# Decoder layer with a mixture of experts: dense routed experts replaced by tokens scattered by expert into 15 tiles

## The reference, cut to what matters

```
shared = einsum(silu(x @ sw_gate) * (x @ sw_up), sw_down)                  # sw_gate, sw_up: 256 x 704
probs  = softmax(x @ router_w.T);  top_w, top_i = top_k(probs, 2)          # 8 experts, two per token
combine = sum(one_hot(top_i, 8) * (top_w / sum(top_w))[..., None])
h = silu(einsum('th,ehi->eti', x, w_gate)) * einsum('th,ehi->eti', x, w_up)   # e = 8, i = 176
routed = einsum('eth,te->th', einsum('eti,eih->eth', h, w_down), combine)
out = x + routed + sigmoid(x @ shared_gate_w)[:, None] * shared
```

## Time and profile before

| what | us |
|---|---|
| median of 3 runs | 638.91 |
| the three runs | 642.28, 638.73, 638.91 |
| span of the profiled execution | 636.7 |
| the profiled execution's own time, taken as the median | 638.9, 2.2 of it around the span |
| group 0's mixer, with no FFN beside it | 0 to 131 |
| mixers of groups 1, 2 and 3, each with an FFN beside it | 131 to 279, 279 to 426, 426 to 572 (ends rounded) |
| tail: the rest of the FFN of group 3 | 572 to 636.7 |

### The profile page before, as it was taken

One profiled execution on the slowest core, in us unless ns is written; L12 is line 12 of the kernel. 1 busy time (PEld: TensorE's weight loads), 2 busy tenths in 40 slices (PEclk: granted clock), 3 DMA queues, 4 the chain that ended last, 5 costly groups with the idle time before them and its releaser, 6 DMA issues.

```text
span 636.7 us, 15520 instructions
## 1 busy us (share of the span) xinstructions
PE 599.7 (94%) x6307; PEld 483.6 (76%) x6307; DVE 409.6 (64%) x841; ACT 278.9 (44%) x637; POOL 342.8 (54%) x462
## 2 busy tenths in 40 slices
PE   7987967979999999999999999999999999999997
PEld 6544545636988889755888889864898888899997
DVE  5997897778744755869644755869762655752221
ACT  4867224232335556342435555251435555343332
POOL 7684145247446667614456666615364666519766
PEclk9999999979999999999999999999999999999999
DMA  8931000020121121011021111002011112014320
GB/s 189 343 104 35 1 1 4 0 68 6 39 67 39 43 60 43 14 34 51 30 80 36 39 52 49 23 17 69 18 51 34 39 44 60 29 38 123 97 55 16
DMA packets 41824, 34.08 MB, mean 54 GB/s; under 512 B 9901, under 2 KB 41206, under 8 KB 41754
## 3 DMA queue, kind: packets, MB, share of 16 engines
q1 hardware_dynamic: 39850, 31.27, 18.2%
q10 hardware_dynamic: 1904, 1.84, 0.9%
HBM read 30.92 MB, written 2.17 MB: 52 GB/s over the span
## 4 chain that ended last, share of the span: by engine, by line
PE 37%; DVE 25%; POOL 13%; issue 9%; ACT 9%; SPq 1%; DMA 1%; POOLq 0%; ACTq 0%; DVEq 0%
DVE A L1574 7%; DVE nm L1652 5%; PE bank L1040 5%; POOL hb L625 3%; PE bank L1237 3%; POOL A L714 3%; PE bank L1044 3%; PE bank L1045 3%; PE bank L1046 3%; PE bank L1084 3%; POOL hT L614 2%; PE bank L1164 2%; POOL hT_last L723 2%; PE bank L1086 2%; PE bank L1085 2%
## 5 line engine op out<-in xcount | busy, mean ns | idle before, releaser
L614 POOL TENSOR_TENSOR hT<-hb,hT 128x256 fp32r<-128x256 f32 (+1 forms) x102 | 78.0, 765 | 72.0 <-ACT hT L789 72.0
L625 POOL TENSOR_TENSOR hb<-hb,cwb 128x256 f32<-128x256 f32 (+1 forms) x102 | 77.0, 755 | 68.6 <-DVE hb L1549 68.5
L1549 DVE TENSOR_TENSOR hb<-hb,bank 128x256 f32<-128x256 f32 (+1 forms) x102 | 42.7, 418 | 101.6 <-ACT hb L799 101.6
L789 ACT ACTIVATE hT<-hb 128x256 fp32r<-128x256 f32 (+1 forms) x102 | 42.4, 416 | 126.0 <-POOL hb L625 125.8
L1044 PE MATMUL bank<-xTf,wGh 128*128 128x256 f32 x272 | 82.9, 305 | 0.0
L1574 DVE TENSOR_TENSOR A<-bank,decay 128x512 f32<-128x512 f32 x128 | 77.4, 682 | 6.0 <-PE bank L1153 5.9
L1045 PE MATMUL bank<-xTf,wGh 128*128 128x256 f32 x272 | 76.7, 282 | 0.0
L1046 PE MATMUL bank<-xTf,wGl 128*128 128x256 f32 x272 | 76.5, 281 | 0.0
L1045 PE MATMUL bank<-xTf,wUh 128*128 128x256 f32 x256 | 72.2, 282 | 0.0
L1046 PE MATMUL bank<-xTf,wUl 128*128 128x256 f32 x256 | 72.1, 282 | 0.0
L1044 PE MATMUL bank<-xTf,wUh 128*128 128x256 f32 x256 | 72.1, 282 | 0.0
(11 more groups left out here) (230 smaller groups left out, 1418.3 us busy)
## 6 DMA issues: line engine op xcount, KB each, us to landing
cwb<-cw_rows SPq DMA_DIRECT2D x54, 128.0 KB, 2.9
A<-cw_rows SPq DMA_DIRECT2D x18, 128.0 KB, 4.0
A<-in_x SPq DMA_DIRECT2D x4, 512.0 KB, 4.3
res<-in_x SPq DMA_DIRECT2D x4, 512.0 KB, 4.8
out_x<-res SPq DMA_DIRECT2D x8, 256.0 KB, 2.4
rawG<-in_L_ffn_w_gate SPq DMA_DIRECT2D x2, 704.0 KB, 6.6
rawU<-in_L_ffn_w_up SPq DMA_DIRECT2D x2, 704.0 KB, 6.6
cwb<-cw_rows SPq DMA_DIRECT2D x12, 112.0 KB, 2.6
```

Of the source, the lines that this page charges most:

```text
L614: pool.tensor_tensor(hT[hr, c % 2, 1, :], hb[hr, c % 2, :], hT[hr, c % 2, 0, :].bitcast(F32), ALU.subtract).then_inc(h_lo, 1)
L625: pool.tensor_tensor(hb[hr, c % 2, :], hb[hr, c % 2, :], cwb[hr, c % CWS, :], ALU.mult).then_inc(h_scaled, 1)
L789: act.activation(hT[hidden(n), c % 2, 0, :], hb[hidden(n), c % 2, :], ACT.Copy).then_inc(h_hi, 1)
L1549: tt(h, h, up_part(PS[5 + c % 2], n), ALU.mult).then_inc(gu_used, 1)
```

## The change

The routed experts are no longer computed for all tokens. A group's 512 tokens have 1024 choices of an expert; each choice gets a row in a table `xs_rows` in device memory (HBM) of RT = 15 tiles of 128 rows, ordered by expert, each expert's share rounded up to whole tiles (15 tiles hold any outcome of the routing). For that, PE counts each token's rank within its expert (`rank_tokens`, 8 small matmuls), DVE turns ranks and counts into row numbers `pos` and a table `tab` of each tile's expert (`place_tokens`, nine small operations after the second scores step), and POOL scatters the normed tokens by 8 indirect DMAs (`scatter`, two behind each of the receptances 4 to 7). PE loads the 15 experts into registers once a group (`load_experts`), and addresses the expert's weights by them.

A routed tile goes: SP loads 128 rows (`load_tile`), PE turns them (2 transposes, L1257), ACT makes the high (L922), DVE the low part (L1790); PE makes gate and up at once with the tokens as the stationary operand (6 matmuls of 352 columns, L1270 to L1272); ACT silu (L928), DVE product (L1811, L1812); PE turns the product (L1286, L1287), ACT makes the high (L934), DVE the low part (L1796); PE multiplies by the down weights (5 matmuls of 256 columns, L1298 to L1302); ACT takes the result out (L941), SP stores it to `ys_rows`. At the end POOL gathers each token's two rows by 8 indirect DMAs (`gather`), and DVE adds them with their weights (`routed_out`, 8 operations). The POOL multiplication by routing weights and the DMAs of `cw_rows` go.

The shared expert stays as before, in 12 items. A group now has 27 items and 30 ticks: shared items at ticks 0 to 5 and 22 to 27, tiles at ticks 7 to 21, which is `n4` to `x3a`. `COUNT` puts one tick instead of two at `x{b}a`. Within the mixers the down product of a tile follows one tick behind its gate and up (`down_lag` 1, shared items still 2), in the tail two. Other moves: the receptance buffer `rbd` lies in the memory of `hT`, the context in that of `hb`, POOL makes seven more constants at the start, and a DMA fills `xs_rows` with zeros once. Line numbers from L1100 on in the quoted pieces are those of the changed kernel.

```diff
-    FN = 2 * FB
-    TICKS = FN + 2
+    SFB = -(-SI // P)
+    FN = 2 * SFB
+    RT = 2 * GT // P + E - 1
+    NI = FN + RT
+    TICKS = NI + 3
...
-        COUNT = dict(n0=1, n1=2, n2=2, n3=2, n4=1, n5=1, y0=2, r0=2, r1=1, r2=1, r3=1)
...
+        COUNT = dict(n0=1, n1=2, n2=2, n3=2, n4=1, n5=1, y0=2, r0=1, r1=1, r2=1)
...
-            for p, k in (("a", 2), ("b", 1), ("c", 2)):
+            for p, k in (("a", 1), ("b", 1), ("c", 2)):
...
+            def load_tile(f, r):
+                if r >= 2:
+                    sp.wait_ge(xt_turned, f * RT + r - 1)
+                sp.dma_start(ring[:, r % 2, :], xsD[r * P:(r + 1) * P, :]).then_inc(xs_in[r % 2], 16)
...
+            def scatter(f, q):
+                k, b = q // GB, q % GB
+                if q == 0:
+                    pool.wait_ge(slots_ready, f + 1)
+                    if f == 0:
+                        pool.wait_ge(zero_out, 16)
+                    else:
+                        pool.wait_ge(xs_in[0], 16 * loads_before(f, 0))
+                        pool.wait_ge(xs_in[1], 16 * loads_before(f, 1))
+                pool.indirect_dma_start(out=xsD, out_offset=bass.IndirectOffsetOnAxis(ap=pos[:, k, b:b + 1], axis=0),
+                                        in_=tok2[:, b, :], in_offset=None).then_inc(scattered, 16)
...
+                if n >= TICKS - 4:
+                    gather(f, 2 * (n - TICKS + 4))
+                    gather(f, 2 * (n - TICKS + 4) + 1)
...
+                    if g and u >= 4:
+                        scatter(g - 1, 2 * (u - 4))
+                        scatter(g - 1, 2 * (u - 4) + 1)
...
+            def ffn_tick(f, n, exp_next=False):
+                if high_late(f, n):
+                    high_part(f, shared_at(f, n - 1))
+                if tile_at(f, n) is not None:
+                    tile_high(f, tile_at(f, n))
+                if down_lag(f) == 1 and routed_at(f, n, 1) is not None:
+                    hidden_high(f, routed_at(f, n, 1))
+                if routed_at(f, n) is not None:
+                    silu_routed(f, routed_at(f, n))
+                elif shared_at(f, n) is not None:
+                    silu_shared(f, shared_at(f, n))
+                if exp_next:
+                    act.activation(spare, mhalf[:, 0:1], ACT.Exp).then_inc(exp_table, 1)
+                if down_lag(f) == 2 and routed_at(f, n, 1) is not None:
+                    hidden_high(f, routed_at(f, n, 1))
+                if routed_at(f, n, down_lag(f)) is not None:
+                    take_out(f, routed_at(f, n, down_lag(f)))
...
+            def gate_up_routed(f, r, e):
+                c, t = f * NI + routed_item(f, r), slice((r % 2) * P, (r % 2 + 1) * P)
+                pe.wait_ge(gu_used, c - 1)
+                if f + 1 < NG and r >= 2:
+                    pe.wait_ge(y_out, f * RT + r - 1)
+                pe.wait_ge(xt_hi, f * RT + r + 1)
+                pe.wait_ge(xt_lo, f * RT + r + 1)
+                o = PS[5 + c % 2][:, 0:2 * I].rearrange("p (w n) -> p w n", w=2)
+                for k in range(KC):
+                    ws = bass.ds(e * I, I)
+                    mm(o, xTf[:, 0, k, t], wH[:, :, k, ws], start=k == 0, stop=False, skip_group_check=True)
+                    mm(o, xTf[:, 1, k, t], wH[:, :, k, ws], start=False, stop=False, skip_group_check=True)
+                    last = mm(o, xTf[:, 0, k, t], wL[:, :, k, ws], start=False, stop=k == 1, skip_group_check=True)
+                last.then_inc(gu_ready, 1)
...
+            def down_routed(f, r, e):
+                c = f * NI + routed_item(f, r)
+                if f == 0 and r == 0:
+                    pe.wait_ge(f_hi, SPLITS)
+                    pe.wait_ge(f_lo[1], len(FW) + len(DOWN_PIECES))
+                pe.wait_ge(r_lo, f * RT + r + 1)
+                if r and f + 1 == NG:
+                    pe.wait_ge(y_out, f * RT + r)
+                h2, o = hT[:, c % 2], PS[y_bank(f, r)][:, 0:C]
+                mm(o, h2[:, 0, 0:P], wDf[:, bass.ds(e * C + DH * C, C)], start=True, stop=False, skip_group_check=True)
+                mm(o, h2[:, 1, 0:P], wDf[:, bass.ds(e * C + DH * C, C)], start=False, stop=False, skip_group_check=True)
+                mm(o, h2[:, 0, 0:P], wDf[:, bass.ds(e * C + DL * C, C)], start=False, stop=False, skip_group_check=True)
+                mm(o, h2[0:I2, 0, P:2 * P], wDf[0:I2, bass.ds(e * C + DM * C, C)], start=False, stop=False, skip_group_check=True)
+                mm(o, h2[0:I1, 1, P:2 * P], wDf[0:I1, bass.ds(e * C + DM * C, C)], start=False, stop=True,
+                   skip_group_check=True).then_inc(down_done, 1)
...
             def ffn_tick(f, n):
+                if n == R0[f] - 1:
+                    load_experts(f)
+                if tile_at(f, n) is not None:
+                    turn_tile(f, n)
+                if down_lag(f) == 1 and routed_at(f, n, 1) is not None:
+                    turn_hidden(f, routed_at(f, n, 1))
+                r = routed_at(f, n)
+                if r is not None:
+                    gate_up_routed(f, r, expert_of[f][r])
+                elif shared_at(f, n) is not None:
+                    gate_up(f, shared_at(f, n))
+                if down_lag(f) == 2 and routed_at(f, n, 1) is not None:
+                    turn_hidden(f, routed_at(f, n, 1))
+                r = routed_at(f, n, down_lag(f))
+                if r is not None:
+                    down_routed(f, r, expert_of[f][r])
+                if n >= 2 and shared_at(f, n - 2) is not None:
+                    down(f, shared_at(f, n - 2))
...
+            def tile_low(f, r):
+                dve.wait_ge(xt_hi, f * RT + r + 1)
+                t = slice((r % 2) * P, (r % 2 + 1) * P)
+                tt(xTf[:, 1, :, t], PS[xt_bank(f, r)][:, 0:KC * P].rearrange("p (k t) -> p k t", k=KC), xTf[:, 0, :, t].bitcast(F32),
+                   ALU.subtract).then_inc(xt_lo, 1)
+
+            def hidden_low(f, r):
+                c = f * NI + routed_item(f, r)
+                dve.wait_ge(h_hi, c + 1)
+                tt(hT[:, c % 2, 1, :], PS[ht_bank(f, r)][:, 0:2 * P], hT[:, c % 2, 0, :].bitcast(F32), ALU.subtract).then_inc(r_lo, 1)
...
+                if n == SFB + 1:
+                    shared_out(f, 0)
+                if tile_at(f, n) is not None:
+                    tile_low(f, tile_at(f, n))
+                if down_lag(f) == 1 and routed_at(f, n, 1) is not None:
+                    hidden_low(f, routed_at(f, n, 1))
+                r = routed_at(f, n)
+                if r is not None:
+                    c = f * NI + routed_item(f, r)
                     dve.wait_ge(silu_done, c + 1)
-                    h = hb[hidden(n), c % 2, :]
-                    tt(h, h, up_part(PS[5 + c % 2], n), ALU.mult).then_inc(gu_used, 1)
+                    h, up = hb[:, c % 2, :], PS[5 + c % 2][:, I:2 * I]
+                    both = h[:, P:P + I2].rearrange("p (w n) -> p w n", w=2)[:, ::-1, :]
+                    tt(h[:, 0:P], h[:, 0:P], up[:, 0:P], ALU.mult)
+                    tt(both, h[:, P:I].unsqueeze(1).to_broadcast([P, 2, I1]), up[:, P:I].unsqueeze(1).to_broadcast([P, 2, I1]),
+                       ALU.mult).then_inc(gu_used, 1)
...
+                    if g and u == 1:
+                        place_tokens(g - 1)
...
+                if g:
+                    routed_out(g - 1, 0)
+                    routed_out(g - 1, 1)
...
-            for n in range(4, AHEAD):
-                gate_up(NG - 1, n)
-            for n in range(FN):
-                if n + AHEAD < FN:
-                    gate_up(NG - 1, n + AHEAD)
-                down(NG - 1, n)
+            for n in range(TICKS):
+                ffn_tick(NG - 1, n)
...
+            place_tokens(NG - 1)
+            for n in range(TICKS):
+                ffn_tick(NG - 1, n)
+            routed_out(NG - 1, 0)
+            routed_out(NG - 1, 1)
```

667 lines of the change are left out of this document (406 added, 261 removed).

## The result

The changed kernel takes 757.25 us in the median of 4 runs (751.06 to 760.04), the kernel before 640.6 (638.73 to 643.61): ratio 1.180, 95% interval 1.173 to 1.187. Forecast were 713, slower.

The account below looks back on a forecast made before the run. PE's matmuls were taken as the bound before the change. Base 636.7 + 58.5 (three middle groups) + 2.0 (start) + 14 (tail) = 711.2 span, plus 2.2 to the median: 713 us; 8-in-10 range 645 to 785.

Parts of the forecast that it names:

- about 19 us a batch, limited by the way through the four engines: X phase: each batch grows from 16.1 to about 19 us, with PE waiting on work passing through the other engines.
- another 1.0: X batch, after the first tick behind the keys: PE's next turning waits 1.0 us for DVE's product.
- the clock: X phase: PE's waits lower its clock, a batch goes to about 26 us; 797, or 755 if half do; chance 0.13.
- 2.08: PE's price in us for one routed tile: six 352-column matmuls, five of 256 columns and four transposes.
- The 1.0 taken: N phase: PE's loading of 15 registers once a group costs 1.0 us, within bounds of 0 and 2.9.
- the 1.2 taken: Scores: one scatter holds POOL 1.2 us, within bounds of 0.39 and 2.9, costing +0.6 for the phase.
- rival 4: A scatter or gather holds POOL the whole 2.9 us, in scores and tail: 780; chance 0.08.
- +2.0: Start: seven more constants on POOL ahead of the decay's cut, 0.29 each, lengthen the start by 2.0 us.
- six shared items to 580: Tail: PE works through six shared items until 580 us while the eight scatters run, also to 580.
- Scores, n and r phase: Additions per middle group: scores +2.0 for placing and +0.6 for scatters, n phase +2.0, r phase +3.9.
- the right sign: X batches of 17 to 21 us, PE idle about 5 us in each; tail's first tile about 21 us after routing starts.
- the wrong signs: X batches under 15 us, PE over 90% busy or clock 0.50 through the x phase, or receptances waiting for POOL's scatters.

Follow-up runs that it names:

- the first experiment: Changed kernel with the hidden tile's turning and high and low parts in each x batch's first tick issued ahead of the previous batch's attention: 729.1 us.
- the fixed experts: Changed kernel with tile r always taking expert r modulo 8, without register loads and address instructions: 749.0 us.
- the full rows: Changed kernel with a tile's last two down matmuls on all 128 rows, not 96 and 48, using the first part's weights: 736.9 us.

## Why the prediction was right, and where its sizes were off

**The direction and the mechanism.** The step "about 19 us a batch, limited by the way through the four engines" came out as 20.6, with its two waits at the named instructions, 2.19 and 1.75 against 2.5 and 1.9; the third, "another 1.0", was 0.3. The three middle groups gave +84 against +58.5. The x batches carry the larger share of this difference: 21.0 against 15.9 before, each on the mean of nine, 5.0 more where the forecast had 2.9 (19 against 16.1), which in these nine makes 19 of the 26 us. With the waits filled and the clock at 1.00 a batch took 19.3. That this is so near 19 is partly luck: four tiles cost 1.1 more than was taken, and the three waits 1.2 less.

**The clock.** It was made a rival, "the clock", that was to bring 7 us per batch; the sum had nothing for it in the x phase. It lies between: in group 2's batches the waits of 2.2 were followed by 0.50, but for some 3 us only, and filling the waits gave 1.7 per batch. The argument by length of wait (1.8 left it at 1.00, 2.5 might not) did not hold up: in the first experiment waits of 1.74 were followed by 0.50 in six of nine batches.

**The price of a tile.** The term "2.08" is 2.35 in the tail, without waits; the fixed experts show that registers have no part in it, the full rows that the change of rows does: it costs 0.35, and the rest of a tile came out 0.08 cheaper than forecast. 0.27 for 60 tiles is 16 us of PE's time. With it the gain of PE is 46.6 - 35.3 = 11.3 per group and not 15.4.

**Registers.** The 1.0 taken is not seen on PE. By the Trainium skill ("Runtime: NRT & Kernel Launch", section "Instruction fetch mechanics") a register takes about 200 ns to load, which gives an estimate of 3.0 us a group for 15; this trace does not show it: the turning behind the load starts 0.12 after the matmul ahead of it. Leaving the loads out brought 8 us in all, which no row assigns to them.

**Scatters.** A scatter holds POOL 0.98 and 0.30 until the next, 1.28 against the 1.2 taken. PE waited for a receptance only once, 1.2 us, so rival 4, POOL's queue, didn't come.

**Start.** "+2.0" was 9.8. Up to the last of group 0's maxima it was 3.8 (97.2 before, 101.1 now), where the sum had 2.0 for the constants. Of the other 6.0, DVE's norm beside POOL's splits and receptances takes 4.7: the step left out that the receptances, free of their old buffer, no longer wait.

**Tail.** 18.6 against 14. The step "six shared items to 580" beside the scatters failed: their low parts wait on POOL behind all eight, 7.6 us of PE, and moving them gave 8 back. The first tile came 25.4 us after the routing's first step, where 21 was the sign.

**Scores, n and r phase** were forecast at 8.5 together. The way from the routing to the first maxima grew by 5.5 to 9.3 and that from the last maxima to the routing by 4.4 to 6.1, the latter with most of the last batch in it. Between the first score product (L1395) and the query projection (L1500) lie 9.2, 6.2 and 4.0 of it, where scores and n phase had 4.6. PE's wait ahead of the scores was 3.44 against 3.7, but not where the forecast had it: the rank matmuls (L1341) did not wait in groups 1 and 2; the projection ahead of them (L1187) waits for DVE's addition of the values (L1730), which stands behind the additions of the gathered rows and the routing:

```profile
317.43 3.68 PE L1187 MATMUL bank<-A,wA 128*128 128x512 f32 x4 [3.44 <-DVE A L1730]
```

Moving half of that addition shortened the wait and left the median as it was. The rest was not taken apart by a run of its own, and its causes stay open.

**Sums.** Some sums of the forecast are slightly off, with no weight in the result: three batches of 19 and one of 17 make 74 and not 75.5, 648 is 11.3 over 636.7 and not 11.5, and with batches of 13.8 the sum would give 651 and not 653.

**The signs.** Three of the nine batches are over the 21 of the right sign, PE is idle 4.1 in a batch and not 5, and none of the wrong signs came: PE is busy 80% of the x phase, at a clock of 0.92.

## What to carry to other kernels

Work taken from the engine that sets the time is a gain only if the waits that this work covered are covered by something else: lay out one period of the program by each engine's order before counting matmuls saved. When a step must be read back in the period in which it was made, put it ahead of the long operations of its engine, and count what the next wait will be: taking away the second wait of a batch and moving the values brought nothing, where 16 and 7 us were expected. And look at what stands behind a slow queue entry and what a freed buffer lets run early: low parts behind the scatters cost 8 us, and a norm took 4.7 longer beside POOL's splits and receptances.

## What the runs showed of the hardware

An idle stretch of PE of 2.2 us was followed by 0.50 of the clock for about 3 us; with 1.9 us of it filled with idle products the clock stayed at 1.00, and a kernel with more matmuls became 25 us faster. Idle stretches of 1.74 to 1.75 were followed by 0.50 in six batches and by 1.00 in three of the same kernel. Of matmuls with 256 columns, the one on 48 rows starts 0.21 after that on 96, and the next one on 128 rows 0.32 after that on 48; on 128 rows throughout they start 0.12 apart, and on 64 rows throughout too. Four DVE operations of 128x256 (L1681, from SBUF to SBUF) take 1.38 with POOL idle, and 4.72 and 6.08 with POOL's 128x512 splits and receptances beside them. Register-addressed weights cost a tile nothing that the tail's tick shows.
